# A graph kernel's front pass: the last two of ten Relus move from ScalarE to GpSimd

## The reference

```python
def _layernorm(x, axis=-1, eps=1e-05):
    m = jnp.mean(x, axis=axis, keepdims=True)
    v = jnp.var(x, axis=axis, keepdims=True)
    return (x - m) / jnp.sqrt(v + eps)
...
h = jnp.maximum(_layernorm(x, axis=-1), 0.0)
...
k = (x @ Wk + bk).reshape(n, H, C)
v = (x @ Wv + bv).reshape(n, H, C)
```

## Time and profile before

| | |
|---|---|
| runs before | 1616.99 us median of 3 (1613.55 to 1619.93) |
| the profiled execution | 1618.57 us |
| its span, first to last instruction | 1616.8 us |
| mean granted clock of TensorE | 0.973 of full |
| busy, share of the span | PE 91%, DVE 80%, ACT 66%, POOL 68% |
| Relus of the front pass | 400, of 0.48 to 0.50 us, in the first 294 us |

### The profile page before, as it was taken

One profiled execution on the slowest core, in us unless ns is written; L12 is line 12 of the kernel. 1 busy time (PEld: TensorE's weight loads), 2 busy tenths in 40 slices (PEclk: granted clock), 3 DMA queues, 4 the chain that ended last, 5 costly groups with the idle time before them and its releaser, 6 DMA issues. The chain is left out here.

```text
span 1616.8 us, 34575 instructions
## 1 busy us (share of the span) xinstructions
PE 1466.4 (91%) x10645; PEld 1264.7 (78%) x10646; DVE 1295.8 (80%) x3599; ACT 1059.3 (66%) x2601; POOL 1097.5 (68%) x1226
## 2 busy tenths in 40 slices
PE   5888889799999999999999965899999898899998
PEld 4666767689999999999999964777777777777776
DVE  8987766269999999999999994677777777677776
ACT  5777879666766677666776613656656665656664
POOL 2566455377777777777777716777777777777774
PEclk9999999889999999999999997999999999999999
DMA  8998998646666666667666626677676667677673
GB/s 218 277 294 269 300 290 286 195 130 190 187 197 182 195 192 188 196 183 196 188 190 196 170 78 163 141 171 166 163 170 161 160 160 170 138 175 165 161 170 97
DMA packets 153580, 303.88 MB, mean 188 GB/s; under 512 B 94658, under 2 KB 98270, under 8 KB 148552
## 3 DMA queue, kind: packets, MB, share of 16 engines
q1 hardware_dynamic: 111443, 200.39, 43.0%
q0 software_dynamic: 41984, 101.72, 25.7%
HBM read 197.23 MB, written 104.50 MB: 187 GB/s over the span
## 5 line engine op out<-in xcount | busy, mean ns | idle before, releaser
L905 POOL DMA_INDIRECT sb_kv<-x_rows,sb_src_all x500 | 473.2, 946 | 191.3 <-issue 109.1
L875 POOL DMA_INDIRECT sb_kv<-kv_rows,sb_src_all x500 | 476.7, 953 | 178.1 <-issue 134.9
L1821 ACT ACTIVATE sb_hn<-sb_xn 100x128 f32<-100x128 f32 x500 | 240.4, 481 | 260.1 <-DMA sb_kv<-x_rows,sb_src_all 219.5
L1824 ACT ACTIVATE sb_vw<-sb_kv 128x128 f32<-128x128 f32 x500 | 239.6, 479 | 0.0
L1733 ACT ACTIVATE sb_hn<-sb_xn,sb_nstat 100x128 f32<-100x128 f32 x500 | 229.9, 493 | 0.0
L1908 PE MATMUL ps_b<-sb_w,sb_memberT 128*125 128x256 f32 x800 | 205.0, 396 | 19.0 <-DVE sb_xn L995 9.7
L1495 DVE COPY sb_hT<-ps_b 128x400 f32<-128x400 f32 x250 | 142.4, 570 | 94.0 <-PE ps_b L2137 93.7
L1908 PEld LDWEIGHTS ps_b<-sb_w,sb_memberT 128*125 128x125 f32 x800 | 148.8, 196 | 42.2 <-issue 15.3
L2137 PE MATMUL ps_b<-sb_member,sb_vw 128*128 128x100 f32 x1000 | 173.4, 277 | 0.0
L2137 PEld LDWEIGHTS ps_b<-sb_member,sb_vw 128*128 128x128 f32 x1000 | 156.7, 197 | 9.8 <-issue 9.8
L2136 PE MATMUL ps_b<-sb_ident,sb_hn 100*128 100x100 f32 x500 | 129.0, 258 | 33.1 <-ACT sb_vw L1824 32.5
(11 more groups left out here) (208 smaller groups left out, 3132.3 us busy)
## 6 DMA issues: line engine op xcount, KB each, us to landing
kv_rows<-sb_kv SPq DMA_DIRECT2D x26, 1120.0 KB
sb_xn<-x_rows SPq DMA_DIRECT2D x50, 507.8 KB
sb_xn<-in_x SPq DMA_DIRECT2D x50, 500.0 KB
out_rows<-sb_xo SPq DMA_DIRECT2D x49, 500.0 KB
x_rows<-sb_xo SPq DMA_DIRECT2D x24, 1015.6 KB
sb_kv<-in_edge_attr SPq DMA_DIRECT2D x500, 32.0 KB
sb_kv<-in_x SPq DMA_DIRECT2D x28, 560.0 KB
kv_rows<-sb_xn SPq DMA_DIRECT2D x13, 1120.0 KB
```

Of the source, the lines that this page charges most:

```text
L875: pool.indirect_dma_start(out=kvs[:, k % 4, t, :], out_offset=None, in_=kv_rows, in_offset=bass.IndirectOffsetOnAxis(ap=src_all[:, n:n + 1 ...
L905: pool.indirect_dma_start(out=xs1[:, k % 4, t, :], out_offset=None, in_=x1, in_offset=bass.IndirectOffsetOnAxis(ap=src_all[:, n:n + 1], ax ...
L1821: nc.scalar.activation(hn1[:, t, :], xn1[:, k % 4, t, 0:D], ACT.Relu, scale=xn1[:, k % 4, t, D:D + 1], bias=xn1[:, k % 4, t, D + 1:XW]).th ...
L1824: nc.scalar.activation(hs1[:, t, :], xs1[:, k % 4, t, 0:D], ACT.Relu, scale=xs1[:, k % 4, t, D:D + 1], bias=xs1[:, k % 4, t, D + 1:XW]).th ...
```

## The change

Tiles 8 and 9 of a block (group 2) are taken from ScalarE and given to GpSimd. For each GpSimd multiplies by the factor and adds the shift, in one instruction; then one more takes the maximum with zero over both tiles. It waits for its own two results in between. TensorE's transposes of group 2 wait for GpSimd, those of groups 0 and 1 for ScalarE. The loads of x wait for both. In GpSimd's queue, before the statistics of pair m stand the two tiles of block 2m - 3, and behind them those of block 2m - 2.

```diff
--- before.py
+++ after.py
@@ -57,6 +57,7 @@
 CELL = 32
 COLS = (BATCHES + QUADS - 1) // QUADS
 N_SOFT = 8
+BY_ACT = 8
 
 T_DVE = (STAT_STEPS + 8 + 1 + STAT_STEPS, 5)
 T_ACT = (3, 2)
@@ -397,6 +398,8 @@
                 self.stat = s("stat_step")
                 self.pool_stat = s("stat_step_by_pool")
                 self.relu = s("relu_done")
+                self.relu_pool = s("relu_done_by_pool")
+                self.part_pool = s("relu_part_by_pool")
                 self.hT = s("h_turned")
                 self.hT_sb = s("h_turned_copied")
                 self.kv = s("kv_ready")
@@ -523,7 +526,8 @@
         @block.sync
         def _(sp):
             def table_load(b):
-                wait(sp, P.relu, B * (b + 1 - X_SLOTS))
+                wait(sp, P.relu, BY_ACT * (b + 1 - X_SLOTS))
+                wait(sp, P.relu_pool, b + 1 - X_SLOTS)
                 rows = x[ROWS * B * b:ROWS * B * (b + 1), :].rearrange("(p t) c -> p t c", t=B)
                 for r in PARTS:
                     sp.dma_start(xp(b)[r, :, :], rows[r, :, :]).then_inc(P.x[b % X_SLOTS], 16)
@@ -838,8 +842,26 @@
                 rows = part_rows.rearrange("(c q s) e -> q s c e", q=QUADS, s=3 * B)[quad, :, 0:cols, :]
                 pool.dma_start(edge_part[CELL * quad:CELL * quad + 3 * B, 0:cols, :], rows).then_inc(edge_part_in, 16)
 
+            def table_relu_last(b):
+                if b < 2 * EARLY:
+                    pool.wait_ge(P.stat, STAT_STEPS * min(b + 1, 3))
+                else:
+                    pool.wait_ge(P.pool_stat, POOL_STEPS * (b // 2 + 1 - EARLY))
+                wait(pool, P.hT, 3 * (b - 1))
+                for t in range(BY_ACT, B):
+                    n = B * b + t
+                    ins = pool.tensor_scalar(hp[:, b % 2, t, :], xp(b)[:, t, :], pstat[:, n, 0:1], pstat[:, n, 1:2],
+                                             ALU.mult, ALU.add)
+                ins.then_inc(P.part_pool, 1)
+                pool.wait_ge(P.part_pool, b + 1)
+                pool.tensor_scalar(hp[:, b % 2, BY_ACT:B, :], hp[:, b % 2, BY_ACT:B, :], 0.0, None, ALU.max
+                                   ).then_inc(P.relu_pool, 1)
+
+            table_relu_last(0)
             for m in range(EARLY, PAIRS):
+                table_relu_last(2 * m - 3)
                 table_stat_math(m)
+                table_relu_last(2 * m - 2)
                 if m % 5 == 4:
                     stats_out(m // 5)
                 if m % 5 == 1 and m > 5:
@@ -859,6 +881,9 @@
                     search_rows()
                 if m == 7:
                     window_pairs()
+
+            for b in range(2 * PAIRS - 3, PB):
+                table_relu_last(b)
 
             def gathers(k):
                 wait(pool, A.vw, k - 3)
@@ -1710,7 +1735,7 @@
             nc.scalar.activation(er[0:1, 0:1], ones[0:1, 0:1], ACT.Exp)
             for b in range(PB + 1):
                 for t in range(B):
-                    if b < PB:
+                    if b < PB and t < BY_ACT:
                         table_relu(b, t)
                     if t == 1 and b > 0:
                         table_turned(b - 1, 2)
@@ -1879,7 +1904,10 @@
             def table_turn(b, g):
                 n = 3 * b + g
                 first, last = FOURS[g]
-                pe.wait_ge(P.relu, B * b + last)
+                if g < 2:
+                    pe.wait_ge(P.relu, BY_ACT * b + last)
+                else:
+                    pe.wait_ge(P.relu_pool, b + 1)
                 wait(pe, P.hT_sb, n - 1)
                 for t in range(first, last):
                     ins = nc.tensor.transpose(banks[n % 2][:, (t - first) * ROWS:(t - first + 1) * ROWS],
```

## The result

| | before | after |
|---|---|---|
| median of the runs made side by side | 1617.43 us (4 runs, 1613.55 to 1619.93) | 1640.18 us (4 runs, 1638.47 to 1645.9) |
| the profiled execution | 1618.57 us | 1638.47 us |
| its span | 1616.8 us | 1636.7 us |
| mean granted clock of TensorE | 0.973 | 0.977 |

The changed kernel is slower by 22.75 us, a ratio of 1.0134 with a 95% interval of [1.0102, 1.0165]. The mechanism is the one forecast. The size was 8 us in the forecast, and slower by more than half a per cent had a chance of 0.46 there, about that of no change (0.47). The measured median is 0.2 us above the stated upper end of 1640 us; as a ratio to before it is just inside it (1.0134 against 1640 by 1616.99, 1.0142).

What follows compares the result with a forecast made beforehand. It took the front pass to be half paced by TensorE's 6.19 us loop, half by late transfers. Stalls of 18 us, less 2.5 in shadow, half given back, left about 8: median 1625 us, range 1612 to 1640.

Steps and rivals of the forecast that it cites:

- The mechanism: Front pass, even blocks: GpSimd's Relus stand behind a new pair's statistics, so TensorE's two-tile transposes wait, 0.9 us a pair.
- The gain of ScalarE: Front pass: 0.8 us a block less Relu work on ScalarE gains 0, since those Relus are outside TensorE's loop.
- Rival (d): Front pass: ScalarE's relief brings Relus 7 and 8 sooner, removing the group 1 wait: 1603 or about 1608 us; chance 0.08.
- The piece R: GpSimd's three new instructions a block, with hand-overs and start, before TensorE's transpose: 1.25 us, between 0.9 and 2.1.
- The 0.26 us for hand-overs and start: Within GpSimd's new work: 0.1 us for each hand-over, to itself and to TensorE, and 0.06 us to start.
- The mean stall of half of what TensorE is early: Even blocks: TensorE is 1.8 us early, successive stalls share it, so 0.9 us a pair, 16.2 us over 18 pairs.
- rival (c): GpSimd's new work collides with VectorE's index work, 2.1 us a block, 1.8 us lost a pair: 1637 to 1642; chance 0.12.
- The lateness of the statistics: Over 18 pairs, GpSimd's statistics end after TensorE wants the even block's transpose: 9.9 us in sum, 0.55 mean.
- The shadow of VectorE from 30 to 80 us: VectorE's index work paces the front pass for two pairs there, hiding some 2.5 us of stalls.
- Half of the remaining stalls given back by the transfers: Front pass: a later TensorE waits less for late x, taking back half of 15.5 us, leaving about 8.
- Rival (b): Transfers pace the front pass and absorb all stalls, or GpSimd's pieces are shorter: about 1618, 1612 to 1621; chance 0.34.
- The odd blocks behind the gathers: GpSimd's Relus behind DMAs: block 9 2.5 us late at no cost, block 13 about 1.4; 2 us put for odd blocks.

Runs made afterwards that it cites:

- the relief alone: Kernel before, with ScalarE leaving out the Relus of tiles 8 and 9, done by no engine; TensorE transposes tiles 6 and 7 again: 1622.22 us, 0.9997.
- light-load traces: Kernels before and after, each with only the first of a block's ten x tiles loaded from block 6 on: 1603.54 us and 1636.51 us.
- the two kernels with the copy moved: ScalarE's copy of group 0 behind Relus 7 and 8: in the kernel before, 1617.45 us; in the changed kernel with GpSimd's Relus one block forward, 1622.36 us.

## Why the prediction was right, and where its size was off

**The gain of ScalarE was priced at 0: right.** The waits for its Relus are 14.7 us against 14.0, the relief alone measured 0.9997, and the block stayed at 6.19 us. Rival (d) has fallen. It needed the copy of group 0 to wait for ScalarE, and the copy waits for TensorE.

**The mechanism, statistics ahead of the even block's Relus: right.** TensorE waits for GpSimd 17 times. When the order alone is changed the waits and the loss go.

**The piece R, forecast at 1.25 us, was 1.89: this term of the sum was mis-sized.** The two multiplications and additions were taken at 0.29 us each from the affine select, and are 0.448; the maximum was taken at 0.41 and is 0.861. The step that failed is the choice of the affine select as "the nearest" row: its slope of 0.92 ns a column in the earlier trace rows was carried to another operation. The 0.26 us for hand-overs and start, for which the prediction had no row, came out smaller: 0.09 us between the multiplications (36.14 and 0.89 long) and the maximum (37.12), 0.05 between its end (37.98) and the transpose (38.03), and no start. Here a maximum of 256 columns takes 861 ns and a multiplication and addition of 128 takes 448, so if both have one price, it is about 3.2 ns a column (413 by 128). The estimate of 1.9 us, and a time near 1635, which the prediction made from the two-input rule in "GPSIMD Engine Reference" of the Trainium skill, § Engine selection, came nearer than the value taken. These instructions read one tensor each, so the rule on one-input work does not agree with the trace, and the measurement decides. For scale, VectorE's addition of two inputs over 512 columns (L1020) takes 683 ns in the mean, 1.3 ns a column.

**The mean stall of half of what TensorE is early: failed with it.** The prediction halved the 1.8 us, since VectorE has 0.85 us in hand and a stall moves the next deadline. R alone does not explain the miss: put into the forecast's own sum, R = 1.89 gives 18 x 1.22 = 22 us of stalls, 24 with the 2 for odd blocks, 21.5 behind the shadow, and a loss of 10.8, not 22.75. With R = 1.89 TensorE is 0.55 + 1.89 = 2.44 us early, more than twice what VectorE has in hand, and the formula of the prediction's rival (c) comes close: 2.44 - 0.85 = 1.6 us a pair, 18 x 1.6 = 29, where the even blocks' stalls are 30.6 in sum. With the 4.9 us of the two odd blocks (2.36 and 2.51) it would be 34; the light-load traces differ by 33.9. The sum agrees better than its parts, for three stalls are missing and others are of 3 us and more. (The lateness of the statistics, 9.9 us in the prediction, adds up to 8.8 when the 18 pairs are taken again from the trace, 0.49 us in the mean. That changes nothing here.) So the size was rival (c)'s (1637 to 1642, chance 0.12), and its cause was not: the instructions are simply long, with minimum and median near each other, and the same work without the wait costs nothing that can be told.

**The shadow of VectorE from 30 to 80 us: mostly wrong.** The prediction hid 2.5 us there. The window of the kernel after (columns as in the earlier trace rows) reads:

```profile
30.00:80.00 50.00, 39.73 (x206) 30.60 (x204) 42.79 (x119) 30.38 (x72) 35.47 (x58) 1.00 0.87 266
```

VectorE did 4.0 us less work in these 50 us than before (42.79 against 46.75), and TensorE 4.1 less. The stalls up to block 8 are 9.0 us in sum, and block 8's two-tile transpose starts at 82.68 where it started at 75.09, 7.6 us later. So little of them was hidden.

**Half of the remaining stalls given back by the transfers: right in kind, and somewhat less in size.** Against the light-load kernels a third of the loss is given back. Put as the prediction put it, stalls of 35.5 us made the pass 19.0 us longer, so 46% of them was given back in the trace, by transfers and shadow together. The wait for x during block 8, four blocks ahead of its use, shows it. VectorE's row of the kernel after, which answers to the first of the earlier trace rows:

```profile
88.98 0.49 DVE L991 BATCH_NORM_STATS2 sb_st<-sb_kv 125x6 f32<-125x128 f32 x2 [3.88 <-DMA sb_kv<-in_x]
```

It comes 5.3 us later than at 83.72 and had still waited 3.88. The load itself was issued later, because it waits until the buffer has been read: the two loads of x on either side of the DMA to `edge_rows` in SP's queue start at 67.74 and 75.55 us, and in the kernel before at 60.85 and 72.47. Transfers that wait for the same stalls as TensorE can hide only a part of them. Rival (b), that they take in all, has fallen.

**The odd blocks behind the gathers:** forecast 2.5 and 1.4 us late, measured 2.36 and 2.51. The first was said to cost nothing, and the two traces agree. The two-tile transpose is 7.6 us later than before at block 8, 10.2 at block 9 and 7.3 at block 10 (91.44 against 81.28, 101.69 against 94.43), so the 2.36 us, and the 3.72 us of block 10 with them, fall into time that the kernel before lost there anyway: from block 9 to block 10 it takes 13.15 us (94.43 less 81.28), against 6.19 undisturbed. At block 13 the transpose is 11.5 us later (125.65 against 114.20), and at block 22 still 11.4 (193.39 against 182.02).

**Smaller points.** ScalarE's busy time fell by 28 us and not by 39: 80 instructions of 0.48 us overlap their neighbours, and leave about 0.36 us each when they go. The maximum takes 0.86 us, outside the 0.25 to 0.45 us that the prediction gave for a call. The sign of being wrong that the prediction named, stalls over 25 us in sum, is what came, with 35.5. The granted clock did not fall as it feared: 0.977 against 0.973 over the whole, 0.98 against 0.95 from 0 to 320 us.

**What stays open.** The spread of the single stalls (0.37 to 3.72 us) was not derived pair by pair. Where the 4.9 us between the two kernels with the copy moved arise is not known. No version tried is clearly faster than the kernel before; the nearest is the one with the copy behind the Relus, 0.9979 [0.9955, 1.0002].

## What to carry to other kernels

Before work is moved to an engine that is idle on average, find what stands ahead of it in that engine's queue, and take the time from the end of that to the moment at which the result is wanted. Here one change of order was worth 20 us, and the 39 us of instructions taken off ScalarE nothing, because they were not in the loop. Where the new operation has no row, let a small run or a neighbour of the same kind price it, and ask of a stall not only how long it is but whether the slack behind it still covers it: past that point, here, each us of the piece cost 15 to 16 us over the 18 pairs.

## What the runs showed of the hardware that was not expected

GpSimd's plain arithmetic is slow by the column. A multiplication and addition with two columns of scalars over 125 x 128 float32 takes 448 ns, a maximum over 125 x 256 takes 861 ns (843 at least), where the affine select over 1000 columns of the earlier trace rows took 1094.

After a long stall TensorE's next matmuls can run at a lower granted clock: it is 0.66 from 193 to 198 us, part of that stretch being at the lower of the two levels (1.2 and 2.4 GHz), and 1.00 from 188 to 193 and from 198 to 202. TensorE's timeline of the kernel after, a stall of 3.23 us and the projection behind it, and the same projection one block on:

```profile
193.39 0.68 PE L1913 MATMUL ps_b<-sb_ident,sb_q 125*128 125x125 f32 x2 [3.23 <-POOL sb_q L857]
193.86 3.36 PE L1936 MATMUL ps_b<-sb_w,sb_memberT 128*125 128x256 f32 x8
...
201.51 1.89 PE L1936 MATMUL ps_b<-sb_w,sb_memberT 128*125 128x256 f32 x8
```

Eight records take 3.36 us instead of 1.89, 1.5 us more on top of the stall. The same is seen behind the stalls of 3.72, 2.83 and 3.21 us at 101.69, 223.37 and 254.77 (granted clock 0.57 from 101 to 105 us, 0.64 from 223 to 227, 0.61 from 254 to 258). The stall of 3.40 us at 38.03 had no such effect (1.00 from 38 to 42 us, the eight records in 1.89 us), so length alone doesn't decide.
